# A second mixture of experts computed by tokens sorted into 15 blocks of one expert each

## The chip, the cores and the metric

The kernel runs on one core of one Trainium2 chip. The metric is the device time of one execution in microseconds (us). The kernel before was timed three times: 1374.06, 1376.27 and 1376.67 us, median 1376.27.

## The reference

Two transformer-like layers run over x of 8 batches, 512 tokens and 128 features, in float32. Each layer has a mixer and a mixture of experts, and in front of each stands a layer norm with a scale and a shift per batch. Layer 0 has causal attention (8 heads) and a small mixture (8 experts of 64). Layer 1 has a state-space mixer (a scan over 512 tokens, 256 channels, 16 states) and the mixture that the change is about, with 8 experts of 512:

```python
logits = xf @ gate_w                      # 128 -> 8 experts
top_w, top_idx = top_k(logits, 2)
top_w = softmax(top_w)
# per token: sum over its two experts e of
#   top_w * (gelu(xf @ w1[e] + b1[e]) @ w2[e] + b2[e])
x = x + gb * that_sum
```

Only two of the eight experts count for a token. Which two depends on the data.

## The kernel before

A batch of 512 tokens is the unit of work. Every engine has its order of work written out by hand. `main(b)` on TensorE is the attention of batch b (32 units of head and query tile), its attention output, layer 0's experts, and the projections and the short convolution of layer 1. `scan(b)` is the state-space scan. The experts of layer 1 belong to batch b-1 when `main(b)` and `scan(b)` run. They are cut into pieces and placed in the gaps, so each engine works on two batches at once (in `main(b)` also on the projections of b+1).

In the kernel before, every token passes through all 8 experts. `hid1(b, n)` (L598) is one hidden chunk: 128 features to 128 hidden units, all 512 tokens, 32 chunks in a batch. ScalarE takes it with a Gelu and its bias (`gelu1`, L929). `out1(b, n)` (L605) is one expert's output for one tile of 128 tokens, four products of 128x128x128, 32 of these in a batch. VectorE adds each output, times its gate, to `expert_sum` (`add_expert`, L1165, four at a time), and `finish` (L1177) multiplies with the layer's gate and adds the residual. A float32 product shows as two matmul records. All expert weights stay in SBUF; they are loaded once by ScalarE's DMA queue (`LATE`, L921).

The pieces lie in these places. In `main`, `early(e, ...)` puts hidden chunks and outputs between the steps of batch b. In `scan`, `SCAN_HIDDEN`, `SCAN_OUTPUT`, `SCAN_GELU` and `SCAN_ADD` name them by state. A Gelu among the scan's exponentials costs ScalarE two table loads (L1084, L1087). The router of batch b-1 runs inside the attention of batch b (`PE_HEAD`, `ACT_HEAD`, `DVE_HEAD` give its units).

In the scan VectorE does for each of 16 states two `tensor_tensor_scan` (L1482) and one product with C (`read_product`, L1156). It needs an exponential per half state from ScalarE (`decays`, L1074, three banks in a ring), an input product from GpSimd (`inject_state`, L435, three buffers), and a broadcast of C from TensorE (L872). GpSimd's products need B broadcast over all partitions: SyncE writes 16 rows to DRAM and reads them back broadcast, two states at a time (`spread_rows`, L395, three buffers). SyncE's queue also places the attention keys (`place_keys`, L372). GpSimd loads x, gates weights, sums half of the scan's output (L466) and stores the output.

After the last batch's scan nothing is left to run beside its experts: router, 32 hidden chunks and 32 outputs form a tail.

## Time and profile before

| What the page says | Value |
|---|---|
| runs | 1374.06 to 1376.67 us, median 1376.27 |
| span of the profiled execution | 1379.8 us |
| TensorE matmul busy | 1207.2 us, 87% |
| VectorE busy | 1037.0 us, 75% |
| ScalarE busy | 852.2 us, 62% |
| GpSimd busy | 489.3 us, 35% |
| moved by DMA | 53.22 MB, mean 39 GB/s |

The page has no time of its own for the profiled execution beside the span. Busy is the time in which an engine ran an instruction. The span covers the whole kernel, in which stages with different limits follow each other; eight batches make about seven equal periods with a head and a tail. Times in the rows below are us from the start of the span, unless a column says otherwise.

### The profile page before, as it was taken

The page shows a single profiled execution, that of the slowest core. Times are in us where ns is not written, and L with a number is a line of the kernel's source. Part 1 is how long each engine was busy: PE and PEld are TensorE (multiplying, and loading weights), DVE is VectorE, ACT ScalarE, POOL GpSimd, SP SyncE. Part 2 cuts the span into 40 slices and gives each one's busy share as a digit, 9 for nine tenths or more (in the row PEclk, how much of TensorE's full clock was granted, in tenths as well). Part 3 has the DMA queues.
Part 4 walks back from the last instruction along what each step waited for, and adds up shares of the span by engine and source line. Part 5 has one row for each costly group of instructions (what it writes and reads, how often), then busy time and mean ns, then how long its engine had stood idle before and what let it go on. Part 6 is the DMA issues. An engine that isn't in the chain of part 4 may idle for free. (4 is left out here: it accounts for less than half of the span.)

```text
span 1379.8 us, 19465 instructions
## 1 busy us (share of the span) xinstructions
PE 1207.2 (87%) x6560; PEld 760.5 (55%) x6560; DVE 1037.0 (75%) x2381; ACT 852.2 (62%) x1600; POOL 489.3 (35%) x309
## 2 busy tenths in 40 slices
PE   5974689989998889989999889989899899889698
PEld 3651145655665556555656456655656556555456
DVE  3666977599866997589866997579975998569822
ACT  2634446488646966489565866479664876469332
POOL 0103930078002950069100960049300870029300
PEclk8995579999999999999999999999999999999899
DMA  7101100030001200020001200021000300011000
GB/s 245 70 16 64 60 8 1 16 108 16 16 17 55 69 12 6 16 92 31 17 9 43 88 1 17 16 78 47 16 1 16 109 16 9 1 64 60 8 1 8
DMA packets 18514, 53.22 MB, mean 39 GB/s; under 512 B 4976, under 2 KB 5864, under 8 KB 18032
## 3 DMA queue, kind: packets, MB, share of 16 engines
q1 hardware_dynamic: 16112, 43.40, 9.8%
q0 software_dynamic: 1296, 4.20, 1.0%
q10 hardware_dynamic: 1008, 4.38, 0.8%
q8 instruction: 53, 0.87, 0.3%
q14 instruction: 45, 0.37, 0.1%
HBM read 45.40 MB, written 2.38 MB: 35 GB/s over the span
## 5 line engine op out<-in xcount | busy, mean ns | idle before, releaser
L1482 DVE TENSOR_TENSOR_SCAN probs_T<-bank,probs_T 128x512 f32<-128x512 f32 x256 | 303.9, 1212 | 16.1 <-ACT bank L1078 12.1
L618 PEld LDWEIGHTS bank<-w_w,hidden 128*128 128x128 f32 x2048 | 248.8, 192 | 72.9 <-issue 66.8
L602 PE MATMUL bank<-hT,w_w 128*128 128x512 f32 x512 | 262.9, 629 | 27.1 <-ACT hidden L933 26.2
L447 POOL TENSOR_TENSOR probs_T<-step_space,probs_T 128x1024 f32<-128x1024 f32 x120 | 282.2, 2358 | 5.9 <-DVE probs_T L1482 5.7
L618 PE MATMUL bank<-w_w,hidden 128*128 128x128 f32 x2048 | 251.6, 276 | 2.1 <-DVE expert_sum L1174 1.6
L933 ACT ACTIVATE hidden<-bank,w_b 128x512 f32<-128x512 f32 x256 | 169.6, 686 | 117.5 <-PE bank L602 116.9
L1006 ACT ACTIVATE probs<-bank,row_neg 128x128 f32<-128x128 f32 (+3 forms) x256 | 134.8, 528 | 151.7 <-DVE row_neg L1335 134.8
L1078 ACT ACTIVATE bank<-step_space,a_neg 128x512 f32<-128x512 f32 x256 | 167.8, 683 | 55.0 <-DVE probs_T L1482 36.7
L701 PE MATMUL bank<-k_pad,q_lat 128*128 128x512 f32 (+3 forms) x512 | 185.3, 448 | 5.8 <-DMA k_pad<-xc 5.8
L1335 DVE TENSOR_REDUCE row_neg<-bank 128x1 f32<-128x128 f32 (+3 forms) x256 | 123.5, 487 | 85.1 <-PE bank L703 82.7
L602 PEld LDWEIGHTS bank<-hT,w_w 128*128 128x128 f32 x512 | 89.0, 194 | 153.0 <-ACT hidden L933 97.0
L466 POOL TENSOR_TENSOR step_space<-step_space,probs 128x512 f32<-128x512 f32 x112 | 142.1, 1269 | 66.2 <-DVE probs L1162 66.1
L663 PE MATMUL bank<-probs,w_ident 128*128 128x512 f32 x256 | 146.0, 654 | 9.1 <-DVE probs L1162 9.1
L1162 DVE TENSOR_TENSOR probs<-probs_T,bank 128x1024 f32<-128x1024 f32 x128 | 153.2, 1197 | 0.4 <-PE bank L663 0.3
L711 PE MATMUL bank<-w_ident,probs 128*128 128x128 f32 x640 | 112.7, 278 | 8.6 <-DVE probs_T L1344 7.8
L1174 DVE SCALAR_TENSOR_TENSOR expert_sum<-bank,gates,expert_sum 128x128 f32<-128x128 f32 x256 | 71.4, 341 | 64.0 <-PE bank L618 62.5
L472 POOL TENSOR_TENSOR gated_out<-w_out_w,gate 128x256 f32<-128x256 f32 x8 | 5.8, 722 | 285.0 <-DVE xn L1214 285.0
L711 PEld LDWEIGHTS bank<-w_ident,probs 128*128 128x128 f32 x640 | 69.9, 142 | 59.1 <-issue 31.0
L872 PE MATMUL bank<-split,select 96*128 96x512 bf16 x128 | 52.7, 412 | 48.5 <-DVE probs L1162 45.7
L701 PEld LDWEIGHTS bank<-k_pad,q_lat 128*128 128x128 f32 x512 | 82.4, 200 | 14.8 <-issue 14.0
L982 ACT ACTIVATE probs_T<-bank 128x128 f32<-128x128 f32 (+3 forms) x176 | 73.8, 420 | 18.3 <-PE bank L711 17.5
L445 POOL TENSOR_TENSOR probs_T<-step_space,probs_T 128x512 f32<-128x512 f32 x16 | 23.3, 1459 | 169.3 <-DVE step_space L1471 169.3
(183 smaller groups left out, 1577.6 us busy)
## 6 DMA issues: line engine op xcount, KB each, us to landing
probs_T<-b_rows_dram SPq DMA_DIRECT2D x64, 512.0 KB, 3.7
w_w<-in_w_dram ACTq DMA_DIRECT2D x2, 2048.0 KB, 14.0
k_pad<-xc SPq DMA_DIRECT2D x64, 64.0 KB, 2.0
x_in<-in_x_dram POOLq DMA_DIRECT2D x8, 256.0 KB, 3.3
gate<-gate_rows_dram SPq DMA_DIRECT2D x1, 2048.0 KB, 7.0
out_dram<-x_out POOLq DMA_DIRECT2D x7, 256.0 KB, 2.8
step_space<-in_wmod_dram SPq DMA_DIRECT2D x1, 768.0 KB, 5.6
probs_T<-in_wqT_dram SPq DMA_DIRECT2D x1, 512.0 KB, 4.1
```

The source lines that it names most:

```text
L447: ins = nc.gpsimd.tensor_tensor(inject[:, n % 3, :, :], u[:], row.unsqueeze(1).to_broadcast([P, DH, T]), ALU.mult)
L466: ins = nc.gpsimd.tensor_tensor(state_sum[:, 1, :], state_sum[:, 1, :], read[:, n % 2, 1, :], ALU.add)
L602: mm(hid1_bank(n)[:], w["w1"][:, n // C1, n % C1 * P:(n % C1 + 1) * P], hT[3][:], start=True, stop=True).then_inc(hid1_mm.sem, 1)
L618: ins = mm(to[:, t * P:(t + 1) * P], hidden[:, (e * C1 + c) % (2 * C1), t * P:(t + 1) * P], w["w2"][:, e * C1 + c, :], start=(c == 0), sto ...
L663: mm(bank[SUM_BANK][:], ident[:], read[:, n % 2, 0, :], start=(n == 0), stop=(n == NS - 1)).then_inc(sum_mm.sem, 1)
L701: mm(s[:, 0:(i + 1) * P], q_lat[:, g, i * P:(i + 1) * P], k_pad[:, g, j, 0:(i + 1) * P], start=True, stop=False)
L711: ins = tr(bank[4 + n % 2][:, k * P:(k + 1) * P], probs_ring[:, n % 4, k * P:(k + 1) * P], ident[:])
L933: f(hidden[:, n % (2 * C1), :], hid1_bank(n)[:], ACT.Gelu, bias=w["b1"][:, n:n + 1]).then_inc(hid1_act.sem, 1)
L1006: f(probs_ring[:, n % 4, 0:(i + 1) * P], bank[SCORE_BANK[n % 4]][:, 0:(i + 1) * P], ACT.Exp, bias=row_neg[:, n % 4:n % 4 + 1], accum_out=r ...
L1078: f(decay(k)[:], delta[:, c, :], ACT.Exp, scale=a_neg[:, c, n:n + 1]).then_inc(dec_ok.sem, 1)
L1162: tt(read[:, n % 2, :, :], state[:, n % 2, :, :], bank[C_BANK][:].unsqueeze(1).to_broadcast([P, DH, T]), ALU.mult).then_inc(rd_ok.sem, 1)
L1482: v.tensor_tensor_scan(state[:, n % 2, c, :], decay(DH * n + c)[:], inject[:, n % 3, c, :], 0.0, ALU.mult, ALU.add).then_inc(st_ok.sem, 1)
```

## The change

The 512 tokens times two choices of a batch (1024 rows) are sorted by expert into blocks of 128 slots, each block belonging to one expert. Because each expert's rows are rounded up to whole blocks, 15 blocks are always enough (`NB = 2 * T // P + E - 1`), and all 15 are always computed.

- Router: `weigh` no longer forms gates for layer 1. TensorE counts ranks with five small bfloat16 products (a triangle and ones against the picks). VectorE's `give_slots` (12 small instructions, most of them waiting for the one before) turns ranks into a slot for each row, an expert for each block (`owner_int`) and a one-hot selection (`own`).
- GpSimd scatters the normalised rows with 8 indirect DMAs into `slots_dram` (`send_rows`). SyncE reads them back in 4 groups ("quads", `fetch_slots`). TensorE transposes a quad and ScalarE modulates it (`("quad", q)` of `FILLS`).
- For each block SyncE reads the expert's number into a register and fetches 512 KB of weights into a ring of 4 (`fetch_expert`; from the fifth block on it waits until the block that used the place is done).
- `fill` and `results` compute a block: a bias product in bfloat16 and 4 products 128x128x128, a Gelu over 128x512, a bias product and 4 products. ScalarE copies a quad of results to SBUF (`take_results`), and SyncE writes it to `results_dram` (`save_slots`).
- GpSimd gathers both rows of each token with 8 indirect DMAs (`collect_rows`) and combines them in 4 instructions (`combine`: 128x1024, then three of 128x512). For the last batch VectorE does this in two halves.
- Removed: `add_expert`, `finish`, the gate transposes and the b2 products (L652, L657), the copy L1322, the loads of w1 and w2 (4 MB), and the expert pieces between the first two projections of batch b+1.
- At the start: 8 new small weight arrays instead of b1 and b2, a memset and a DMA that clear `slots_dram` ahead of the first `place_keys`, and 15 small VectorE instructions in the set-up.

`_upto(n)` is the index behind block n in `FILLS`, and `_done(n)` is its `results`. The core of the diff, with indentation taken off and blank lines left out:

```diff
+def fetch_expert(b, n):
+    if n == 0:
+        sp.wait_ge(owner_ok.sem, owner_ok.at(b, 1))
+    if n >= WR:
+        sp.wait_ge(block_mm.sem, block_mm.at(b, n - WR + 1))
+    elif b > 0:
+        sp.wait_ge(block_mm.sem, block_mm.at(b - 1, NB))
+    e = sp.value_load(owner_int[0:1, n:n + 1], min_val=0, max_val=E - 1)
+    sp.dma_start(expert_w[:, n % WR, :],
+                 io["experts"][bass.ds(e, 1), :, :].rearrange("a p f -> (a p) f")
+                 ).then_inc(expert_in[n % WR].sem, 16)
...
+def start_experts(b):
+    for n in range(WR):
+        fetch_expert(b, n)
+    fetch_slots(b)
...
+if behind:
+    for n in SP_EXPERTS.get(p, ()):
+        fetch_expert(b - 1, n)
+    for q in SP_SAVES.get(p, ()):
+        save_slots(b - 1, q)
...
+def send_rows(b):
...
+for k in range(2):
+    for t in range(NT):
+        pool.indirect_dma_start(
+            out=slots_dram[:, :], out_offset=bass.IndirectOffsetOnAxis(ap=slot[:, k, t:t + 1], axis=0),
+            in_=xn_slots[:, t, :], in_offset=None).then_inc(spread.sem, 16)
...
+if b >= 2:
+    collect_rows(b - 2)
+if b < B - 1:
+    load(b + 1)
+if b >= 2:
+    combine(b - 2)
+    store(b - 2)
+send_rows(b - 1)
...
+    mm(to[:].rearrange("p (c s) -> p c s", c=C1), bias1[:],
+       own[:, n, :].unsqueeze(2).to_broadcast([96, C1, P]), start=True, stop=False, skip_group_check=True)
+    i = n % QUAD
+    for c in range(C1):
+        ins = mm(to[:, c * P:(c + 1) * P], expert_w[:, n % WR, c * P:(c + 1) * P],
+                 slots_T[:, n // QUAD % 2, i * P:(i + 1) * P], start=False, stop=(c == C1 - 1),
+                 skip_group_check=True)
+ins.then_inc(fill_mm.sem, 1)
...
+mm(to[:, i * P:(i + 1) * P], own[:, n, 0:1].to_broadcast([96, P]), bias2[:],
+   start=(i == 0), stop=False, skip_group_check=True)
 for c in range(C1):
-    ins = mm(to[:, t * P:(t + 1) * P], hidden[:, (e * C1 + c) % (2 * C1), t * P:(t + 1) * P],
-             w["w2"][:, e * C1 + c, :], start=(c == 0), stop=(c == C1 - 1))
-ins.then_inc(out1_mm.sem, 1)
+    ins = mm(to[:, i * P:(i + 1) * P], hidden[:, n % HR, c * P:(c + 1) * P],
+             expert_w[:, n % WR, F1 + c * P:F1 + (c + 1) * P], start=False, stop=(c == C1 - 1),
+             skip_group_check=True)
+ins.then_inc(block_mm.sem, 1)
...
+    ins = f_(slots_T[:, n % 2, 0:m], fill_bank(f)[:, 0:m], ACT.Identity,
+             bias=mod[:, 1, 3, bass.ds(b, 1)], scale=mod[:, 1, 4, bass.ds(b, 1)])
+else:
+    if n >= HR:
+        act.wait_ge(block_mm.sem, block_mm.at(b, n - HR + 1))
+    ins = f_(hidden[:, n % HR, :], fill_bank(f)[:], ACT.Gelu)
...
+def take_results(b, q, tail=False):
+    n = quad_size(q)
+    act.wait_ge(block_mm.sem, block_mm.at(b, q * QUAD + n))
+    if b > 0 or q >= 2:
+        act.wait_ge(saved[q % 2].sem, saved[q % 2].at(b, 16 * (q // 2)))
+    f_(slots_out[:, q % 2, 0:n * P], bank[TAIL_BANK[q] if tail else SLOT_BANK[q]][:, 0:n * P], ACT.Copy
+       ).then_inc(slots_done.sem, 1)
...
-stt(expert_sum[:, t, :], source[:, t * P:(t + 1) * P], gates[1][:, t, e:e + 1],
-    expert_sum[:, t, :], ALU.mult, ALU.add).then_inc(out1_add.sem, 1)
...
+link(tt(over[:], total.unsqueeze(2).to_broadcast([P, E, NT]),
+        limits[:].unsqueeze(1).to_broadcast([P, E, NT]), ALU.is_gt))
+link(v.reduce_sum(blocks[:], over[:], AX_X))
+link(v.tensor_tensor_scan(ends[:], w["unit"][:], blocks[:], 0.0, ALU.mult, ALU.add))
+mark(tt(starts[:], ends[:], blocks[:], ALU.subtract))
+link(tt(passed[:], ends[:, 0:E - 1].unsqueeze(1).to_broadcast([P, NB, E - 1]),
+        firsts[:].unsqueeze(2).to_broadcast([P, NB, E - 1]), ALU.is_le))
+mark(stt(place[:], starts[:].unsqueeze(1).to_broadcast([P, NT, E]), float(P), rank, ALU.mult, ALU.add))
+link(v.reduce_sum(owner[:], passed[:], AX_X))
+cp(owner_int[:], owner[:]).then_inc(owner_ok.sem, 1)
+link(tt(placed[:].rearrange("p k t e -> p k (t e)"), picks[:].rearrange("p k t e -> p k (t e)"),
+        place[:].rearrange("p t e -> p (t e)").unsqueeze(1).to_broadcast([P, 2, NT * E]), ALU.mult))
...
+FILLS = [("quad", 0)]
+for _n in range(NB):
+    FILLS.append(("block", _n))
+    if _n % QUAD == 1 and _n // QUAD + 1 < NQ:
+        FILLS.append(("quad", _n // QUAD + 1))
...
+PE_EARLY = (_fills(0, 3) + _done(0) + _fills(3, _upto(2)) + _done(1) + _fills(_upto(2), _upto(3)),
+            _done(2),
+            _fills(_upto(3), _upto(4)),
+            _done(3),
+            [],
+            _done(4) + _fills(_upto(4), _upto(6)))
+PE_SCAN = {1: _done(5) + _fills(_upto(6), _upto(7)), 2: _done(6) + _fills(_upto(7), _upto(8)),
+           4: _done(7) + _fills(_upto(8), _upto(9)), 5: _done(8) + _fills(_upto(9), _upto(10)),
+           7: _done(9) + _fills(_upto(10), _upto(11)), 8: _done(10) + _fills(_upto(11), _upto(12)),
+           10: _done(11) + _fills(_upto(12), _upto(13)), 11: _done(12) + _fills(_upto(13), _upto(14)),
+           13: _done(13), 14: _done(14)}
+ACT_EARLY = (_fills(0, _upto(3)), _fills(_upto(3), _upto(4)) + [("results", 0)])
+ACT_SCAN = {2: _fills(_upto(4), _upto(6)), 8: _fills(_upto(6), _upto(8)),
+            12: [("results", 1)], 14: _fills(_upto(8), _upto(10)), 20: _fills(_upto(10), _upto(12)),
+            24: [("results", 2)], 25: _fills(_upto(12), _upto(14)), 31: [("results", 3)]}
...
+SP_EXPERTS = {"head": (4, 5, 6, 7), 1: (8,), 3: (9,), 4: (10, 11), 5: (12,), 6: (13,), 7: (14,)}
+SP_SAVES = {1: (0,), 5: (1,), "end": (2, 3)}
```

`PE_EARLY[k]` stands where `early(...)` stood in `main`: 0 ahead of the third layer norm's transposes, 1 behind them, 2 in the middle of the four input projections, 3 behind them, 5 behind the dt products. `ACT_EARLY[0]` stands ahead of the third modulation, and `ACT_EARLY[1]` between the two `xi` and the two `res_gate` activations, ahead of their table load.

## Rows read from the trace of the kernel before

**Rows 1.** Windows of one steady period: us, busy per engine, clock, DMA share, GB/s.

```profile
600.60:662.30 61.70, 55.02 (x250) 33.59 (x250) 59.09 (x69) 51.60 (x66) 53.43 (x30) 0.97 0.14 49
662.30:706.50 44.20, 39.75 (x289) 26.78 (x288) 36.83 (x127) 27.62 (x94) 2.81 (x3) 1.00 0.04 13
706.50:738.90 32.40, 31.46 (x184) 20.16 (x184) 18.61 (x79) 13.86 (x22) 2.68 (x3) 1.00 0.07 18
738.90:759.00 20.10, 18.92 (x94) 12.14 (x92) 13.30 (x24) 14.73 (x23) 2.11 (x2) 1.00 0.21 63
```

**Rows 2.** Groups by line: out<-in, count, busy us, mean ns, idle before.

```profile
L1482 DVE TENSOR_TENSOR_SCAN probs_T<-bank,probs_T 128x512 f32<-128x512 f32 x256 | 303.9, 1212 | 16.1 <-ACT bank L1078 12.1 <-POOL probs_T L445 1.5 <-POOL probs_T L447 1.1
L447 POOL TENSOR_TENSOR probs_T<-step_space,probs_T 128x1024 f32<-128x1024 f32 x120 | 282.2, 2358 | 5.9 <-DVE probs_T L1482 5.7
L602 PE MATMUL bank<-hT,w_w 128*128 128x512 f32 x512 | 262.9, 629 | 27.1 <-ACT hidden L933 26.2 <-ACT hT L939 0.9
L618 PE MATMUL bank<-w_w,hidden 128*128 128x128 f32 x2048 | 251.6, 276 | 2.1 <-DVE expert_sum L1174 1.6
L933 ACT ACTIVATE hidden<-bank,w_b 128x512 f32<-128x512 f32 x256 | 169.6, 686 | 117.5 <-PE bank L602 116.9
L872 PE MATMUL bank<-split,select 96*128 96x512 bf16 x128 | 52.7, 412 | 48.5 <-DVE probs L1162 45.7 <-DVE split L1463 2.7
```

**Rows 3.** VectorE's timeline of one scan: start, us, line, instructions, idle before.

```profile
600.63 1.22 DVE L1482 TENSOR_TENSOR_SCAN probs_T<-bank,probs_T 128x512 f32<-128x512 f32 x1
...
603.18 1.10 DVE L1174 SCALAR_TENSOR_TENSOR expert_sum<-bank,gates,expert_sum 128x128 f32<-128x128 f32 x4
...
608.25 2.34 DVE L1482 TENSOR_TENSOR_SCAN probs_T<-bank,probs_T 128x512 f32<-128x512 f32 x2 [1.56 <-ACT bank L1078]
...
662.32 1.21 DVE L1162 TENSOR_TENSOR probs<-probs_T,bank 128x1024 f32<-128x1024 f32 x1
```

**Rows 4.** TensorE's granted clock early in that scan, columns as in rows 1.

```profile
604.00:606.00 2.00, 2.00 (x4) 0.68 (x3) 1.93 (x4) 1.16 (x2) 2.00 (x2) 0.54 0.33 127
```

**Rows 5.** Timeline of the attention: one of finish's two instructions, the b2 products.

```profile
668.66 0.68 DVE L1181 TENSOR_TENSOR expert_out<-expert_sum,gate 128x512 f32<-128x512 f32 x1
...
696.76 1.15 PE L657 MATMUL bank<-w_b,gates_T 8*128 8x128 f32 x8
```

**Rows 6.** TensorE's timeline: last projection, and the third layer norm's transposes.

```profile
729.10 1.00 PE L638 MATMUL bank<-w_wv_down,hT 128*128 128x64 f32 x8
...
738.90 0.60 PE L586 MATMUL bank<-w_ident,xn 128*128 128x128 f32 x4
```

**Rows 7.** ScalarE's timeline between the input projections and the convolution's output.

```profile
743.12 1.26 ACT L933 ACTIVATE hidden<-bank,w_b 128x512 f32<-128x512 f32 x2
744.39 1.28 ACT L1052 ACT_TABLE_LOAD   x1
...
747.21 1.23 ACT L1060 ACTIVATE xc<-probs_T 128x512 f32<-128x512 f32 x2 [0.25 <-DVE probs_T L1450]
```

**Rows 8.** DMA issues (KB each, us to landing), and GpSimd's time for an issue.

```profile
probs_T<-b_rows_dram SPq DMA_DIRECT2D x64, 512.0 KB, 3.7
out_dram<-x_out POOLq DMA_DIRECT2D x7, 256.0 KB, 2.8
...
L430 POOL DMA_DIRECT2D out_dram<-x_out x7 | 5.6, 796 | 37.3 <-DVE x_out L1184 37.3
```

**Rows 9.** The chain that ended last: start, us, what.

```profile
1309.56 3.78 PE bank L602 x4
...
1314.60 0.20 DVE logits L1222
...
1366.70 7.16 PE bank L618 x64
...
1375.70 0.72 POOL out_dram L523
```

**Rows 10.** TensorE's first score of batch 0.

```profile
28.78 0.76 PE L701 MATMUL bank<-k_pad,q_lat 128*128 128x128 f32 x2 [5.82 <-DMA k_pad<-xc]
```

More of the change, by code:

```diff
@@ L364, in build @@
         first_a, first_b = FIRST
-        then = [name for name in w if name not in LATE + first_a + first_b]
+        then = [name for name in w if name not in first_a + first_b]
         n_first, n_weights = len(first_a) + len(first_b), len(then)
@@ L622, in project, with pieces @@
+            def pieces(b, names, tail=False):
+                for kind, n in names:
+                    if kind == "fill":
+                        fill(b, n)
+                    else:
+                        results(b, n, tail)
             def project(b, k):
@@ new lines, in _upto, with _done @@
+def _upto(n):
+    return FILLS.index(("block", n)) + 1
+def _done(*blocks):
+    return [("results", n) for n in blocks]
+PE_EARLY = (_fills(0, 3) + _done(0) + _fills(3, _upto(2)) + _done(1) + _fills(_upto(2), _upto(3)),
[9 more added lines that the diff above has]
+           13: _done(13), 14: _done(14)}
```

559 lines of the change are left out of this document (340 added, 219 removed).

## The prediction

> **What bounds the kernel now.** I read the windows of one steady period first, then the groups by line, then the timelines of VectorE, TensorE and ScalarE in that period, the DMA issues, and last the chain at the end. The reader is to see in [rows 1] that the four stages have different limits. In the scan VectorE is busy 59.1 of 61.7 us, TensorE 55.0 and GpSimd 53.4. In the attention nobody is full (TensorE 39.8, VectorE 36.8 of 44.2): it is a chain from TensorE to VectorE to ScalarE and back. From 706.5 to 738.9 TensorE is full (31.5 of 32.4). The last 20.1 us are a serial chain into the next scan. A period is 158.4 us. In the tail TensorE is alone and full [rows 9].
>
> **The work saved, and why it is not the gain.** The dense experts cost TensorE (262.9 + 251.6) / 8 = 64.3 us a batch [rows 2]. The 15 blocks have 120 products of 128x128x128 at 251.6 / 1024 = 0.246 us, 29.5 us, with 15 wide and 15 narrow bias products (at most 0.41 and some 0.1 us, by L872) and 15 transposes (0.15 us each, by L586): 39 us. TensorE loses 25 us a batch. Gelus fall from 32 to 15 at 686 ns, with 8 quad passes added. The gain is only what lies on each stage's limit.
>
> **The scan.** VectorE loses six groups of four adds at 1.10 us [rows 3], five inside and one just ahead: 6.6 us. Given back: about 1.0, since GpSimd starts from the same operand and its first products (2.36 us, L447) now set the first states. At half state 2 ScalarE takes block 5, quad 2 and block 6 in one visit, but block 6 needs quad 2 modulated first, and TensorE's broadcast of C for state 0 is queued behind block 6. The sequence is a table load, Gelu, modulation, TensorE 1.2 us, Gelu, table load, against four Gelus before, where VectorE waited 1.56 us [rows 3]. TensorE also stands idle for some 6 us ahead of it, and the clock already dips there (0.54, [rows 4]). I take 2.5 us more wait. The visit at half state 14 has the same form one time more, 0.6. Net -2.5 us; bounds -6.6 (all hidden) and +1. GpSimd's 53.4 us of products and sums forbid much more.
>
> SyncE is in order: each row pair of B now stands behind fetches that wait for blocks. The worst is pair 4 behind experts 10 and 11 (block 7, placed at state 4). It would land about 13 us later than now, where GpSimd has some 11 us of slack, so GpSimd is 2 to 3 us late, which its lead over VectorE covers. At nothing, then, and 2 to 4 us a batch if the cover is gone.
>
> **Scan to attention.** The last group of adds (1.10) goes, but TensorE's last sum hides most of it: -0.4.
>
> **Attention.** Removed: finish (2 x 0.68), the b2 products (1.15, [rows 5]) and their copy (0.68). Added on VectorE: 12 small instructions at about 0.2, 2.4 us, all linked. On GpSimd, which is busy 2.8 of 44.2 us, 16 indirect DMAs and 6.2 us of combining (2.36 + 3 x 1.27). The router of the next batch waits for the gathers. These start when the scan's last sum is done, take 8 issues and 2 us of landing, and are needed some 22 us later. The scatter must be read back before TensorE's fills some 30 us after the slots. Both hold while an indirect issue costs under 2.5 us. Taken -1.0; bounds -3.2 and +2.4.
>
> **Main.** The two pairs of hidden chunks between the projections go, hidden by a layer norm: -0.5. Then TensorE had 9.8 us from L638 to L586 [rows 6]. New: a wait for v of 0.7, quad 0 and its modulation, blocks 0 to 3 with two results and quad 1: 0.44 + 1.1 + 4 x 1.11 + 2 x 0.95 + 0.44 and the waits give 738.9 again: 0. The layer norm was ready at 734.4, so what could be gained here is refilled.
>
> Then comes an added wait. ScalarE's `results 0` needs block 3, which TensorE does only behind all four input projections. Queued behind it are the silu table load (1.28), two `res_gate` and both `xc` activations, which everything up to the scan waits for. TensorE: projections 0, 1 to 742.2, block 4 to 743.3, projections 2, 3 to 745.1, block 3's results to 746.0. ScalarE: copy to 747.0, table to 748.2, res_gate to 749.5. So xc starts at 749.5, not 747.21, where the slack was 0.25 [rows 7]: +2.3. Bounds: 0 (if the convolution were later too) and +4 (expert 4's weights late at 742.2; they are asked for at about 735.3 and need 3.7 to land [rows 8] and a register read).
>
> A period: -2.5 - 0.4 - 1.0 - 0.5 + 2.3 = -2.1 us, and 7 such: -15 us. Bounds -6 and +2.5 a period.
>
> **The start.** Batch 0's first score waits 5.82 us for the keys [rows 10], whose DMAs stand behind SyncE's weight issues, slowed by the 4 MB of expert weights. These go; six more small arrays and a clear come. Bounds 0 and -5.8, taken -2.5.
>
> **The tail.** The router no longer stands behind two hidden chunks (3.78, [rows 9]): the logits come at 1310.8 instead of 1314.6. Choice 2.8, ranks 0.9, slots 2.1: 1316.6. Then 8 scatters. An indirect issue is nowhere in the trace; bounds 0.80 (GpSimd's issue of a direct one, [rows 8]) and 2.36 (its longest instruction, L447); I take 1.2, nearer the issue. Landing 2.0 (2.8 - 0.8). So 1328.3, read back 2.7: 1331. A block is 16 records at 7.16 / 64 = 0.112 [rows 9] and two biases, 2.1 us. Its weights are asked for when the block four earlier is done, and are needed two blocks later: about 0.9 of issue and register read plus 3.7 of landing over two blocks is 2.3 us each, 34.5 in all. With 2.5 to fill the pipeline and 2 for a low clock after TensorE's idle 15 us: 1370. Copy and save 3.0, gathers 9.6 + 2.0, two halves on VectorE 2 x 2.1: x_out at 1389 against 1375.5. So +13.5, bounds +7 and +38 (24 issues count, 8 of them an earlier batch's).
>
> **Sum.** 1376.3 - 15 - 2.5 + 13.5 = 1372. Durations are from the profiled execution, whose span is 1379.8, 3.5 us over the median of the runs; I carry differences to the median.
>
> **Rivals.**
>
> *The blocks pay more (chance 0.20).* If ScalarE's copy of quad 0 doesn't hold xc and the attention gains its full 3.2, a period gains 2.1 + 2.3 + 2.2 = 6.6 us, but GpSimd holds it to about 5.5: 1376 - 38 - 2.5 + 13.5 = 1349. For it: TensorE has slack everywhere, and its waits shape the attention. Against: the order of the copy is in the code.
>
> *The indirect DMAs are dear (0.18), slower.* Place: scatter and gathers of the tail. 16 issues are bare there, and 8 of the batch before stand ahead of the scatter. At 2.0 us each the tail is 13.5 + 16 x 0.8 + 6 = +32: 1391. It decides from about 1.45 us an issue. For it: each reads an index per row. Against: the direct issue of 512 rows is 0.80.
>
> *Weights or B rows come late (0.14), slower.* SyncE's register read before each fetch at 2 us instead of 0.5 gives the tail 0.75 x 11 = 8 us more, and stalls of 2 us a period in the scan: 1372 + 8 + 14 = 1394. For it: 512 KB take 3.7 us, and 15 fetches share one queue. Against: DMA share is 0.14 in the scan.
>
> *TensorE's clock (0.08), slower.* In the scan TensorE falls from 55 to some 36 busy us of 60, in lumps with idle between. At 1.2 GHz (half) that is 72 us, more than VectorE's. If a third of each scan ran so, states with a block would cost 1 us more, some 3 us a period: 1372 + 21 = 1393. Rows 4 show the clock at 0.54 right after one wait of 2.3 us, and back at 1.00 in the window of the scan (0.97 mean, [rows 1]). The Trainium skill, page "TensorE: Matmul & The Clock Gate", section "HAM oscillation", says that matmul groups shorter than the waits between them start cold each time. By that rule this rival holds in every scan and would take the 21 us; the trace agrees for the one wait only.
>
> **How the numbers follow.** Forecast 0.40 with its own range 1361 to 1383, then 0.20, 0.18, 0.14, 0.08. The range for 8 in 10 is 1346 to 1402. A measurement of this kernel tells 0.2% (2.75 us) from no change. Below 1373.5: 0.28 of the forecast and the first rival, 0.48. Within: 0.09 and 0.04 of the slower ones, 0.13. Above: 0.39.
>
> **What would show it.** Right: the scan's window at 57 to 60 us without L1174; xc starting right behind two res_gate and these behind the copy of quad 0, 2 us later than the convolution; about 17 us in the tail between slots and first fill; the last gathers 10 to 13 us. Wrong: a period shorter by over 5 us or longer at all; POOL indirect issues far from 1.2 us; SyncE waiting for blocks while GpSimd waits for rows; a clock under 0.9 in the scan.

## The result: 4.6% slower, and the profile after

The changed kernel takes 1442.3 us (median of five runs, 1431.0 to 1445.1) against 1376.3: ratio 1.0456, 95% interval 1.0413 to 1.0500. The forecast was 1372 and the range ended at 1402. The profiled execution is the quickest of the five: 1431.0 us, span 1429.2, mean granted TensorE clock 0.879 (before 0.950). In the other four the clock is 0.868 to 0.871. So the stages below add up to 49.4 us where the medians differ by 66.1: the span of 1379.8 is by itself 3.5 us over the median of the kernel before, and 1431.0 is 11.3 us under the median here. Each ratio further down is against the kernel before timed beside it (medians 1375.6 to 1378.9). One execution, of the kernel with both edits, took 1444.2 us at a clock of 0.778 and is left out of its ratio.

I cut both profiled spans at VectorE's own marks: x_mid, the first addition of the attention's output, the addition of out0, the first convolution tap, the first instruction on the x projection (split), the first scan. Sums over the kernel, in us:

| stage | before | after | difference | predicted |
|---|---|---|---|---|
| start to first scan | 128.6 | 119.5 | -9.1 | -2.5 |
| attention (x_mid to its first addition), 7 times | 264.8 | 289.9 | +25.1 | -7 |
| attention to out0, 7 | 140.8 | 145.2 | +4.4 | -3.5 |
| out0 to convolution, 7 | 90.8 | 90.7 | -0.1 | 0 |
| convolution to split, 7 | 57.5 | 76.0 | +18.5 | +16.1 |
| split to scan, 7 | 59.2 | 62.7 | +3.5 | 0 |
| scan to x_mid, 8 | 560.8 | 547.0 | -13.8 | -20.3 |
| x_mid to the end | 77.3 | 98.2 | +20.9 | +13.5 |
| span | 1379.8 | 1429.2 | +49.4 | -4 |

The worst term is the attention, 32 us from where I put it. Its first of the seven, with nothing to combine yet, takes 35.95 us; the other six take 41.0 to 42.8, where the kernel before has 38.0. First the windows of one steady period (us, busy time of each engine, granted clock, DMA share, GB/s), against [rows 1]:

```profile
604.30:665.20 60.90, 45.01 (x229) 30.98 (x229) 55.11 (x51) 42.95 (x60) 53.29 (x30) 0.89 0.35 122
665.20:713.00 47.80, 42.63 (x282) 28.94 (x282) 38.42 (x128) 26.64 (x89) 22.65 (x21) 0.89 0.21 66
713.00:745.60 32.60, 27.98 (x190) 20.39 (x189) 17.56 (x74) 11.20 (x18) 5.63 (x6) 0.95 0.26 75
745.60:768.10 22.50, 14.09 (x73) 8.98 (x71) 13.08 (x19) 14.48 (x22) 1.64 (x1) 1.00 0.45 153
```

The scan's window is 0.8 us shorter than before. The attention's is 3.6 us longer, although VectorE, TensorE and ScalarE do about the same work in it. What is new is GpSimd, 22.65 us busy instead of 2.81, and a clock of 0.89 instead of 1.00. Now VectorE's timeline there, and GpSimd's beside it (start, us, engine, line, instructions):

```profile
680.63 0.69 DVE L1546 TENSOR_REDUCE row_neg<-bank 128x1 f32<-128x512 f32 x1
681.24 0.63 DVE L1489 SCALAR_TENSOR_TENSOR rstd<-newton,rstd 128x4 f32<-128x4 f32 x1
681.90 3.23 DVE L1493 TENSOR_SCALAR xn_slots<-x_mid,meanvar,rstd 128x128 f32<-128x128 f32 x4
```

```profile
678.61 1.89 POOL L583 TENSOR_TENSOR rows<-rows,shares 128x1024 f32<-128x1024 f32 x1 [0.80 <-DMA rows<-results_dram,slot]
680.58 1.27 POOL L588 TENSOR_TENSOR rows<-rows 128x512 f32<-128x512 f32 x1
681.93 1.27 POOL L592 TENSOR_TENSOR x_out<-rows,gate 128x512 f32<-128x512 f32 x1
683.28 1.26 POOL L596 TENSOR_TENSOR x_out<-x_out,x_mid 128x512 f32<-128x512 f32 x1
```

In the kernel before the same step and the same normalisation were:

```profile
678.78 0.15 DVE L1280 SCALAR_TENSOR_TENSOR rstd<-newton,rstd 128x4 f32<-128x4 f32 x1
678.97 1.11 DVE L1283 TENSOR_SCALAR xn<-x_mid,meanvar,rstd 128x128 f32<-128x128 f32 x4
```

The four normalising instructions take 3.23 us instead of 1.11, exactly while GpSimd combines. Taken one by one they last 1.38, 1.42, 0.33 and 0.33: the first two end 0.08 us behind the ends of GpSimd's last two operations, and then the way is free. A step on 4 columns takes 0.63 instead of 0.15, and ends 0.02 behind the GpSimd operation beside it; one at 678.84 takes 1.68. The row maximum out of PSUM, in the same stretch, keeps its 0.69. TensorE waits for the normalised rows, and its clock falls behind the wait (windows of 4 us, same columns as above):

```profile
684.00:688.00 4.00, 1.52 (x10) 1.33 (x11) 3.97 (x11) 2.23 (x8) 1.37 (x2) 0.84 0.22 66
688.00:692.00 4.00, 4.00 (x22) 3.87 (x21) 0.99 (x3) 2.02 (x7) 0.00 (x0) 0.50 0.00 0
692.00:696.00 4.00, 4.00 (x32) 2.04 (x34) 2.83 (x15) 1.27 (x5) 0.00 (x0) 0.50 0.00 0
696.00:700.00 4.00, 4.00 (x37) 2.82 (x30) 2.85 (x12) 1.68 (x8) 0.00 (x0) 0.88 0.00 0
```

VectorE is full in the first window while TensorE works 1.52 of 4 us; for the next 8 us TensorE is full at 0.50 (1.2 GHz) and VectorE waits.

ScalarE behind the input projections, against [rows 7] (in brackets the idle time ahead and what ended it):

```profile
753.21 0.60 ACT L1112 ACTIVATE slots_out<-bank 128x512 f32<-128x512 f32 x1 [2.13 <-PE bank L805]
753.83 1.28 ACT L1230 ACT_TABLE_LOAD   x1
755.12 1.27 ACT L1233 ACTIVATE res_gate<-bank,w_in_b 128x512 f32<-128x512 f32 x2
756.28 1.15 ACT L1238 ACTIVATE xc<-probs_T 128x512 f32<-128x512 f32 x2
```

This is the copy of quad 0's results with the table load and the four activations queued behind it, as predicted. The new groups by line, against [rows 2] (out<-in, count, busy us, mean ns, idle before):

```profile
L1675 DVE TENSOR_TENSOR_SCAN probs_T<-bank,probs_T 128x512 f32<-128x512 f32 x256 | 301.2, 1211 | 39.0 <-ACT bank L1256 28.6 <-POOL probs_T L610 8.6 <-POOL probs_T L608 1.5
L610 POOL TENSOR_TENSOR probs_T<-step_space,probs_T 128x1024 f32<-128x1024 f32 x120 | 281.8, 2355 | 18.8 <-DMA probs_T<-b_rows_dram 16.2 <-DVE probs_T L1675 2.6
L575 POOL DMA_INDIRECT rows<-results_dram,slot x64 | 64.1, 1002 | 66.2 <-issue 66.2
L563 POOL DMA_INDIRECT slots_dram<-xn_slots,slot x64 | 63.0, 985 | 161.6 <-DVE slot L1452 121.1 <-issue 40.5
```

In the scan VectorE waits 39.0 us in all instead of 16.1, most of it for ScalarE's exponentials (28.6 instead of 12.1). GpSimd waits 16.2 us for rows of B, which I had covered "at nothing". An indirect issue is 1.0 us, with 0.30 before the next. Last the tail's chain and the end, against [rows 9], and the first score, against [rows 10]:

```profile
1356.22 2.23 DMA slots_dram<-xn_slots,slot
1358.47 2.83 DMA slots_in<-slots_dram
1361.34 1.13 PE bank L779 x4
...
1400.68 2.32 DMA results_dram<-slots_out
1403.00 1.92 issue
1404.92 0.98 POOL rows L575
...
1413.76 2.47 DMA rows<-results_dram,slot
...
1420.73 0.74 POOL out_dram L695
```

```profile
25.60 0.46 PE L894 MATMUL bank<-k_pad,q_lat 128*128 128x128 f32 x2 [2.59 <-DMA k_pad<-xc]
```

From the last store's issue to the end it is 8.5 us (1429.2 - 1420.7), where the kernel before needs 4.1 (1379.8 - 1375.7). The trace's records show where it goes: GpSimd's last instruction, a DRAIN, takes 5.87 us (1423.15 to 1429.02), and 1.46 in the kernel before.

### The profile page after: what moved, and what is told of

The parts are those of the page before. It is cut to its first block and busy times, and to the rows that moved or that the text cites. A ratio compares the mean times of both kernels' runs of the same rounds, so it can differ in the third digit from the quotient of the medians.

```text
span 1429.2 us, 19661 instructions
## 1 busy us (share of the span) xinstructions
PE 1073.9 (75%) x6224; PEld 728.4 (51%) x6224; DVE 1006.9 (70%) x2193; ACT 755.0 (53%) x1492; POOL 661.1 (46%) x466
## 5 line engine op out<-in xcount | busy, mean ns | idle before, releaser
L1675 DVE TENSOR_TENSOR_SCAN probs_T<-bank,probs_T 128x512 f32<-128x512 f32 x256 | 301.2, 1211 | 39.0 <-ACT bank L1256 28.6
L610 POOL TENSOR_TENSOR probs_T<-step_space,probs_T 128x1024 f32<-128x1024 f32 x120 | 281.8, 2355 | 18.8 <-DMA probs_T<-b_rows_dram 16.2
L1546 DVE TENSOR_REDUCE row_neg<-bank 128x1 f32<-128x128 f32 (+3 forms) x256 | 121.4, 485 | 80.1 <-PE bank L896 78.8
L858 PE MATMUL bank<-probs,w_ident 128*128 128x512 f32 x256 | 156.6, 697 | 9.1 <-DVE probs L1359 9.1
L629 POOL TENSOR_TENSOR step_space<-step_space,probs 128x512 f32<-128x512 f32 x112 | 142.2, 1269 | 40.4 <-DVE probs L1359 40.3
L805 PEld LDWEIGHTS bank<-expert_w,hidden 128*128 128x128 f32 x960 | 130.3, 211 | 33.4 <-issue 32.9
L805 PE MATMUL bank<-expert_w,hidden 128*128 128x128 f32 x960 | 147.1, 301 | 0.0
L790 PEld LDWEIGHTS bank<-slots_T,expert_w 128*128 128x128 f32 x960 | 136.3, 205 | 8.0 <-issue 2.3
L563 POOL DMA_INDIRECT slots_dram<-xn_slots,slot x64 | 63.0, 985 | 161.6 <-DVE slot L1452 121.1
L790 PE MATMUL bank<-slots_T,expert_w 128*128 128x128 f32 x960 | 135.4, 287 | 0.0
L904 PE MATMUL bank<-w_ident,probs 128*128 128x128 f32 x640 | 118.9, 290 | 20.3 <-DVE probs_T L1555 19.0
L1103 ACT ACTIVATE hidden<-bank 128x512 f32<-128x512 f32 x120 | 70.9, 597 | 84.3 <-PE bank L790 83.9
L1050 PEld LDWEIGHTS bank<-split,select 96*128 96x128 bf16 x128 | 13.0, 102 | 166.6 <-DVE probs L1359 162.9
L575 POOL DMA_INDIRECT rows<-results_dram,slot x64 | 64.1, 1002 | 66.2 <-issue 66.2
L786 PE MATMUL bank<-own,bias 96*128 96x512 bf16 x120 | 49.5, 412 | 59.4 <-ACT hidden L1103 50.1
```

What stands on the lines that cost most here:

```text
L610: ins = nc.gpsimd.tensor_tensor(inject[:, n % 3, :, :], u[:], row.unsqueeze(1).to_broadcast([P, DH, T]), ALU.mult)
L629: ins = nc.gpsimd.tensor_tensor(state_sum[:, 1, :], state_sum[:, 1, :], read[:, n % 2, 1, :], ALU.add)
L790: ins = mm(to[:, c * P:(c + 1) * P], expert_w[:, n % WR, c * P:(c + 1) * P], slots_T[:, n // QUAD % 2, i * P:(i + 1) * P], start=False, st ...
L805: ins = mm(to[:, i * P:(i + 1) * P], hidden[:, n % HR, c * P:(c + 1) * P], expert_w[:, n % WR, F1 + c * P:F1 + (c + 1) * P], start=False, ...
L858: mm(bank[SUM_BANK][:], ident[:], read[:, n % 2, 0, :], start=(n == 0), stop=(n == NS - 1)).then_inc(sum_mm.sem, 1)
L904: ins = tr(bank[4 + n % 2][:, k * P:(k + 1) * P], probs_ring[:, n % 4, k * P:(k + 1) * P], ident[:])
```

## The experiments

### GpSimd's combination against VectorE's normalisation

One wait is added in the changed kernel, so that the combination runs behind the normalisation:

```diff
                 if b >= 2:
+                    pool.wait_ge(*nth(ln_xn, b - 1, 3))
                     combine(b - 2)
```

> The changed kernel with one wait more: GpSimd combines the rows of the batch before (four tensor operations, 5.7 us) only after VectorE has normalised x_mid. Collision theory (VectorE's small norm steps and xn_slots are slowed while GpSimd's tensor operations run: xn_slots 3.23 us instead of 1.11, two norm steps 2.3 instead of 0.3, then a low TensorE clock behind the hole): the attention from x_mid to its end falls from 39.3 us to 35 or 36 in six batches, xn_slots is 1.1 us, ratio to the kernel before about 1.03 instead of 1.046. Rival (the attention is long because of the low clock, whose cause is TensorE's smaller load, or because of the gathers): the attention stays over 38 us and the ratio at 1.044 or above.

Measured: 1409.3 us, ratio 1.0204 (1.0162 to 1.0246), 33 us less. The attention is 35.5 to 36.1 us in batches 2 to 7, where it was 41.0 to 42.8: 38.7 us less in all six (the 39.3 of the expectation is no length by these marks), also less than the kernel before (37.98). VectorE and GpSimd there:

```profile
682.68 1.11 DVE L1494 TENSOR_SCALAR xn_slots<-x_mid,meanvar,rstd 128x128 f32<-128x128 f32 x4
```

```profile
683.88 1.89 POOL L583 TENSOR_TENSOR rows<-rows,shares 128x1024 f32<-128x1024 f32 x1 [4.05 <-DVE xn_slots L1494]
```

The same work 5 us later costs nothing. The reverse is the kernel before with such work added, and read by nobody:

```diff
+            def combine_pairs(b):
+                pool.wait_ge(chain_norm.sem, chain_norm.at(b, 7))
+                for k in range(4):
+                    pool.wait_ge(paired.sem, paired.at(b, k))
+                    nc.gpsimd.tensor_tensor(pair[:], pair[:], gate[:, b:b + 1, 3, :].to_broadcast([P, NT, P]),
+                                            ALU.mult if k % 2 == 0 else ALU.add).then_inc(paired.sem, 1)
```

> The kernel before, with four GpSimd tensor operations of 128x512 (1.27 us each) on a buffer of their own added in the attention of six batches, started when seven of the twelve norm steps of x_mid are done; nothing waits for their results. Collision theory: the normalisation (1.11 us) takes 2 to 3.3 us, small norm steps up to 1.7, and each of the six attentions grows by 2.5 to 4.5 us: ratio 1.011 to 1.02. Rival (GpSimd's tensor work costs VectorE nothing; the gathers or the blocks are the cause): ratio 0.998 to 1.002.

Measured: 1402.8 us, ratio 1.0184 (1.0156 to 1.0213). The six attentions grow by 5.1, 2.3, 4.5, 4.5, 2.3 and 4.5 us. Nothing of the blocks is in this kernel, and the normalisation takes the same 3.23 in each of the six:

```profile
686.16 3.23 DVE L1294 TENSOR_SCALAR xn<-x_mid,meanvar,rstd 128x128 f32<-128x128 f32 x4
```

So the same collision costs 2.3 us twice and 4.5 or more four times. The difference goes with TensorE's clock behind it, which stayed at 1.00 in the two and fell in the four. Batches 2 and 3 of this kernel (columns as in [rows 1]):

```profile
368.00:375.00 7.00, 6.47 (x69) 4.98 (x70) 4.83 (x23) 3.90 (x14) 0.00 (x0) 1.00 0.01 4
528.00:535.00 7.00, 6.73 (x35) 5.75 (x39) 3.05 (x13) 3.93 (x14) 0.00 (x0) 0.51 0.01 4
```

Two more runs of this kernel ask what collides. In one the wait is for `ln_xn` instead of the seventh norm step; in the other eleven memsets stand in place of the four operations:

```diff
-                pool.wait_ge(chain_norm.sem, chain_norm.at(b, 7))
+                pool.wait_ge(*nth(ln_xn, b, 3))
```

> The kernel before with the same four GpSimd tensor operations on a buffer of their own in six attentions, but started when x_mid is normalised, so that they stand beside VectorE's maxima and copies out of PSUM. Theory (it matters which VectorE operations stand beside): the normalisation takes 1.11 us, the maxima keep their 0.69 for 512 columns, the attention 37.98 us, ratio 0.998 to 1.003. Rival (any GpSimd work in the attention costs): 2 to 4 us in each of six attentions as in the run with the early start, ratio 1.009 or above.

```diff
-                for k in range(4):
+                for k in range(11):
                     pool.wait_ge(paired.sem, paired.at(b, k))
-                    nc.gpsimd.tensor_tensor(...)
+                    nc.gpsimd.memset(pair[:], 1.0).then_inc(paired.sem, 1)
```

> The kernel before with eleven GpSimd memsets of 128x512 (by the 1.73 us of the 1920-column one about 0.46 us each, 5 us in all) beside the norm steps, in place of the four tensor operations: GpSimd writes and reads nothing. Theory A (each of the four normalising operations waits for the whole GpSimd operation ahead of it, whatever that does): the normalisation takes up to 4 x 0.46 us more, about 2 to 2.9 us instead of 1.11, the 128x4 steps stay at 0.16 or wait up to 0.46; ratio 1.004 to 1.012. Theory B (only operations of GpSimd that read SBUF collide): normalisation 1.11 us, ratio 0.998 to 1.003.

Measured: 1.0003 (0.9982 to 1.0023) behind the normalisation, and 1.0004 (0.9979 to 1.0029) with memsets. VectorE behind the normalisation, with GpSimd at its four operations from 679.55 to 684.87:

```profile
679.38 0.68 DVE L1346 TENSOR_REDUCE row_neg<-bank 128x1 f32<-128x512 f32 x1
...
681.00 0.68 DVE L1355 COPY probs_T<-bank 128x512 f32<-128x512 f32 x1
...
682.37 1.30 DVE L1361 COPY hidden<-row_inv 128x256 f32<-128x256 f32 x1
```

Reads out of PSUM keep their time. The one copy out of SBUF takes 1.30 instead of 0.29, in a place where nobody waits for it. And the normalisation beside the memsets, then the memsets:

```profile
997.79 1.21 DVE L1293 TENSOR_SCALAR xn<-x_mid,meanvar,rstd 128x128 f32<-128x128 f32 x4
```

```profile
676.81 3.56 POOL L520 MEMSET pair<- 128x512 f32 x6 [2.00 <-DVE rstd L1286]
```

0.10 us more in each of the six, the steps on 4 columns keep their 0.15 or 0.16, and the attention is 38.06 us instead of 37.98. Theory B stands as to the cost: beside GpSimd operations that read the four lose 2.1 us, beside pure writes 0.1. They aren't untouched, though. The first and the third normalising instruction take 0.44 and 0.63 us instead of 0.34 and end 0.08 us behind the end of a memset (0.52 us each), but the instruction behind each is through 0.06 to 0.16 us later. The Trainium skill, page "SBUF — State Buffer", section "Who interferes with whom", says that VectorE's second pair of SBUF ports is also GpSimd's only one, that the first to issue holds it for its whole instruction, and that reductions never contend; the rows agree in that VectorE's held instructions end 0.02 to 0.08 us behind the end of a GpSimd operation, and in the 0.69 for the maxima. For a VectorE operation with two inputs in SBUF, as most of the small steps are, the section counts only a GpSimd operation that reads as a rival. For the 2-port modes, which tensor_scalar can enter (no row here shows the mode), it counts GpSimd whatever it does; beside pure writes the runs show 0.10 us, and that measurement decides here.

How much of the 6.6 us is the clock: two products that nothing reads, ahead of the transposes of xn_slots, with the collision left in.

```diff
+                    if behind and n == PE_HEAD[0]:
+                        for _ in range(2):
+                            mm(bank[MISC][:], ident[:], w["wfcT"][:], start=True, stop=True)
```

> The changed kernel, collision left in, with two 128x512 matrix products (0.94 us each) into an unused bank just ahead of the transposes of xn_slots, where TensorE idles 1.6 us. Clock theory (of the 6.6 us that the collision costs, the part beyond VectorE's lost 3.9 us comes from TensorE's granted clock falling to 0.50 behind that idle time): the clock in the 9 us behind stays above 0.9 and the attention falls from 42.5 to about 40 us; ratio about 1.035. Rival (the rest is the chain itself, the clock has no part): attention 42 to 43, ratio 1.043 or above.

Measured: 1436.6 us, ratio 1.0403 (1.0354 to 1.0453), too near the 1.0456 to be told from it. The attention is the cleaner number: 40.3 us in batches 3 to 6 instead of 42.5, with the clock at 0.96 and 0.62 where it was 0.50:

```profile
704.00:708.00 4.00, 2.68 (x21) 2.46 (x22) 2.48 (x8) 3.45 (x13) 0.00 (x0) 0.96 0.15 45
708.00:712.00 4.00, 4.00 (x40) 2.19 (x39) 2.61 (x13) 1.27 (x5) 0.00 (x0) 0.62 0.01 4
```

The two products aren't free: in batch 1, where nothing collides, the attention is 37.6 us instead of 35.95. So at least 2.2 of the 6.6 us are the clock, the same 2.2 by which the collision's price differs in the kernel before, and some 4 are VectorE's lost time (3.23 - 1.11, and two steps at 1.68 and 0.63 instead of 0.3 together, 4.1).

### The indirect DMAs

Eight indirect DMAs become two direct ones. The rows then go to and come from fixed places, so this kernel's experts see other rows.

```diff
-                    for t in range(NT):
-                        pool.indirect_dma_start(...).then_inc(spread.sem, 16)
+                    pool.dma_start(slots_dram[k * T:(k + 1) * T, :].rearrange("(t p) d -> p t d", p=P), xn_slots[:]
+                                   ).then_inc(spread.sem, 16)
```

> The changed kernel with every group of eight indirect DMAs replaced by two direct ones of the same bytes (rows go to and come from fixed places, so the experts see other rows). My theory: indirect issues cost time only where they are bare, in the tail: about 8 us less for the scatter and 8 less for the gathers, nothing in the periods, ratio about 1.034. If the 8.5 us from the last store's issue to the end (4.1 in the kernel before) come from the indirect DMAs, 4 us more go: 1.031. Rival (the gathers, 10 us of GpSimd in every period, slow the attention): 2 us or more less in each period too, ratio 1.024 or below.

Measured: 1403.2 us, ratio 1.0170 (1.0141 to 1.0199), 39 us less: my theory named 20, the rival's "2 us in each period" is nearer. But the gathers are not what slows the attention. Without their 10 us the combination falls onto other norm steps: xn_slots takes 1.12 us in every batch and the attention 38.4 in four of them, 2.5 more than without any collision. That is the collision again, half missed. In the tail the span ends 4.6 us behind the last store's issue instead of 8.5 (last line of its chain; the span is 1403.6):

```profile
1399.04 0.72 POOL out_dram L690
```

The tail from x_mid to the end is 82.7 us instead of 98.2. So 15.5 us of it are the indirect DMAs, of which 3.9 come at the very end of the program, where GpSimd's DRAIN takes 1.95 us instead of 5.87. I had no term for those.

### ScalarE's copy

```diff
-ACT_EARLY = (_fills(0, _upto(3)), _fills(_upto(3), _upto(4)) + [("results", 0)])
+ACT_EARLY = (_fills(0, _upto(3)), _fills(_upto(3), _upto(4)))
...
                     f(xc[:, c, :], conv[1][:, c, :], ACT.Silu).then_inc(xc_ok.sem, 1)
+                if behind:
+                    pieces(b - 1, [("results", 0)])
```

> The changed kernel with ScalarE's copy of the first quad's results moved from ahead of the silu table load to behind both xc activations. By the step of my prediction (2.3 us a period stand between convolution and scan because of this copy): convolution to split falls from 10.5 to 8.2 us in each of the periods with blocks, 14 to 16 us in all, ratio about 1.035. Rival (the copy only moves: TensorE's scan start waits for it as well): the stage split to scan grows by what the first loses, ratio 1.044 or above.

Measured: 1415.9 us, ratio 1.0301 (1.0239 to 1.0363), 26 us less. Convolution to split is 8.56 us in every batch instead of 10.44 to 11.91, which is 16 of it. The scan takes 1.1 us more. In the profiles, attention, attention to out0 and split to scan are 3.5, 3.7 and 3.6 us shorter too, though the edit doesn't touch them; their lengths follow the clock, as the next runs show. With both edits:

> Both edits of the two experiments before: the combination waits for the normalisation, and the first quad's results are copied behind xc. If the two are independent: attention 35.9 us in all six batches, convolution to split 8.56, and split to scan 8.44 throughout, since TensorE's idle time ahead of the x projection is 1.6 us instead of 3.8. From 1409: 7 times (11.3 - 8.6) and about four times 1.8 less, so about 1383, ratio 1.003 (0.998 to 1.010). Rival (what is shortened in one stage comes back in the next): over 1395, ratio 1.013 or above.

Measured: 1390.8 us, ratio 1.0088 (1.0057 to 1.0119); expected 1383. All three stages are at the times named (35.9, 8.56, 8.44), but attention to out0 is 21.8 us instead of 20.8 or 19.5, and the scan 69.1. A miss of a kind that the next runs explain.

### TensorE's clock

The stages between the attention and the scan have two or three lengths each: 19.5, 20.8 or 21.8; 8.44 or 10.23. In the kernel with the combination later, split to scan is 10.23 us in six batches, with these products in it:

```profile
755.49 3.78 PE L1038 MATMUL bank<-proj,w_dt_w 112*128 112x512 f32 x4 [0.78 <-ACT proj L1242]
```

In the profiled run of the changed kernel the same four took 1.99 us:

```profile
759.71 1.99 PE L1037 MATMUL bank<-proj,w_dt_w 112*128 112x512 f32 x4 [0.78 <-ACT proj L1241]
```

In both, TensorE had waited 3.78 us for xc; once the clock was at 1.00 behind it, once at 0.50. Three products into that wait:

```diff
                 early(3)
+                if behind:
+                    for _ in range(3):
+                        mm(bank[MISC][:], ident[:], w["wfcT"][:], start=True, stop=True)
```

> The kernel with the combination later, and in each batch three 128x512 matrix products (2.8 us) into an unused bank where TensorE waits 3.8 us for xc. Clock theory: the dt products (3.78 us at a granted clock of 0.50, 1.98 at 1.00) are always at 1.00, split to scan is 8.44 us in every batch instead of 10.23 in most, conversion to split about 10.4 instead of 11.5; 12 to 20 us less, ratio 1.007 to 1.012 instead of 1.020. Rival (added products delay the x projection or the clock falls all the same): ratio 1.018 or above.

Measured: 1391.1 us, ratio 1.0120 (1.0069 to 1.0170) against 1.0204 (1.0162 to 1.0246), two intervals that just touch: split to scan 8.44 us in seven of the eight batches, convolution to split 10.44 in all seven with blocks. This is also where I see the 11 us between the profiled run of the changed kernel and its median: that run has 8.44 in its first six batches and 10.23 in its last two, and the other runs' clocks are lower. The start can hold as much of it (see there). Their stages are not on record, so this is argued, not shown. Then products in such waits, on top of both edits: ahead of the second layer norm's transposes, of the x projection, of block 6 and of the first score, in this order in the diff:

```diff
+                    for _ in range(2):
+                        mm(bank[OUT_BANK][:], ident[:], w["wfcT"][:], start=True, stop=True)
...
+                for _ in range(1 if behind else 7):
+                    mm(bank[MISC][:], ident[:], w["wfcT"][:], start=True, stop=True)
...
+                    for _ in range(5):
+                        mm(bank[MISC][:], ident[:], w["wfcT"][:], start=True, stop=True)
+                    pieces(b - 1, _fills(_upto(6) - 1, _upto(6)))
...
+            for _ in range(3):
+                mm(bank[0][:], ident[:], hT[0][:], start=True, stop=True)
```

> The kernel with both edits (combination later, results copied behind xc), and 128x512 matrix products into unused banks where TensorE waits: two ahead of the second layer norm's transposes (wait 1.8 us), one ahead of the x projection (1.6), five ahead of block 6 (6.1), three at the start ahead of the first score, seven ahead of batch 0's x projection. Clock theory (what is still lost in the periods is lost at a granted clock of 0.50 behind these waits): attention to out0 19.5 instead of 21.8 in every batch, scan 67 to 68.5 instead of 69.1, first scan at about 119 to 121 instead of 127.9; a period 153.5 instead of 157; about 1361, ratio 0.985 to 0.990. Rival (the clock isn't held by this, or the products delay the real work): ratio 1.005 or above.

Measured: 1368.1 us, ratio 0.9936 (0.9919 to 0.9953). Attention to out0 is 19.48 us in batches 1 to 6 and the scan 67.8 in three of them; batch 7 stayed as it was (22.15), and in batches 2 and 6 the clock fell one stage later, where no products stand (out0 to convolution 14.81 us instead of 13.18), and the scan took 70.5. Hence less than hoped. The first scan came at 127.4 in this profile, of the longest of the seven executions (1377.2), but at 121.4 and 122.1 in the next two kernels, which have the same start. In the tail, twelve and then sixteen products, and the last store but one behind the scatter:

```diff
             expert_head(B - 1, 2)
+            for _ in range(12):
+                mm(bank[6][:], ident[:], w["wfcT"][:], start=True, stop=True)
             pieces(B - 1, TAIL, tail=True)
```

> As the kernel with products in all waits, and in the tail twelve more such products where TensorE waits 17 us for the scattered rows, and the last store but one behind the scatter instead of ahead of it. Clock theory: the first blocks of the tail run at 1.00 instead of 0.50 (4 us less), the scatter starts 0.8 us earlier: 4 to 5 us less than that kernel, ratio 0.982 to 0.987. Rival: the products last until after the rows are there, or the clock has fallen again: the same ratio within 0.002.

> The kernel with products in all waits and sixteen instead of twelve in the tail: the twelve ended 4.7 us before the scattered rows were there, and the granted clock was 0.50 to 0.75 again in the first 8 us of blocks. Clock theory: the wait left is under 1.5 us, the first blocks take 0.9 us of products each instead of 1.7, and the tail from x_mid to the end falls from 99.5 us to 95 to 96: ratio 0.990 to 0.994. Rival (the products run over the landing of the rows, or the tail's blocks are bound by the weights' fetches): tail 98 us or more, ratio 0.995 or above.

Measured: 0.9968 (0.9943 to 0.9994) and 0.9933 (0.9906 to 0.9960), 1369.3 and 1366.8 us. Twelve ended 4.7 us early and gained nothing: the tail was 99.4 us, and 99.2 without them. Sixteen end 1.4 us early, and the tail is 96.5 (the wait for the rows with sixteen):

```profile
1299.00 0.66 PE L780 MATMUL bank<-w_ident,slots_in 128*128 128x128 f32 x4 [1.43 <-DMA slots_in<-slots_dram]
```

The intervals of the three kernels overlap, so the tail's 3 us stand on single profiles.

### The start

In the kernel before, the 4 MB of expert weights go behind the first keys, and then three products into the wait for those keys:

```diff
-            for name in LATE:
-                act.dma_start(w[name][:], io[name]).then_inc(experts_in, 16)
...
                          .to_broadcast([P, B, 4, P])).then_inc(gates_spread, 16)
+            for name in LATE:
+                sp.dma_start(w[name][:], io[name]).then_inc(experts_in, 16)
```

> The kernel before with the two loads of all expert weights (4 MB) moved from ScalarE's queue at the start to SyncE's behind the placing of the first keys and the gates. Theory (the changed kernel's start gains 9 us because these loads no longer fill the DMA engines while the keys are placed, and because TensorE's clock no longer falls to 0.50 behind the wait for them): first score at 25 to 26 us instead of 28.8, first scan at 119 to 121 us instead of 128.6, all the rest as before; ratio 0.993 to 0.995. Rival (the gain has another source, such as the smaller set-up): ratio 0.998 or above.

> The kernel before with the expert weights loaded behind the first keys, and three 128x512 products into an unused bank where TensorE waits 2.6 us for those keys. Clock theory of the start: batch 0's attention runs at a granted clock of 1.00 in every run and the first scan starts at 119 to 120 us instead of 121.8; ratio 0.992 to 0.995, with less spread between runs. Rival (the low clock further on in batch 0 has another cause): ratio 0.996, as without the products.

Measured: 0.9955 (0.9929 to 0.9981), then 0.9943 (0.9924 to 0.9961). The first score is at 25.79 us instead of 28.78 and the first scan at 121.8 instead of 128.6:

```profile
25.79 0.46 PE L703 MATMUL bank<-k_pad,q_lat 128*128 128x128 f32 x2 [2.55 <-DMA k_pad<-xc]
```

So 3 us are the wait and 4 are what follows from it, in these two profiles. The products added nothing in the profile (first scan at 121.5); the two ratios can't be told apart.

The start isn't the same in every execution. The changed kernel and its six variants with the same start (each profiled once) have their first scan at 119.5, 127.8, 126.7, 119.5, 127.9, 133.0 and 122.2 us; the kernel before and the three with GpSimd work added have it at 128.6, 124.3, 128.8 and 128.9. In the profiled execution of the changed kernel the clock stays at 1.00 from 25 to 60 us; with the combination later, same start, it is 0.50 from 28 to 34.

## Why the prediction was wrong

**The step that failed** is the attention's: "On GpSimd, which is busy 2.8 of 44.2 us, 16 indirect DMAs and 6.2 us of combining". I priced this at nothing because GpSimd was free, and forecast -7 us for the seven attentions; they took 25.1 more. GpSimd was free, but its neighbour was not: VectorE had the small norm steps and the normalisation at that moment, and whichever came up beside a GpSimd operation ended only behind it (two steps and two of the four normalising instructions, 4.1 us in a batch). Behind that TensorE's clock fell, which is the other part of the 6.6. The two runs that move only this work (33 us less when it is later, 24 us more when it is added to the kernel before) show it from both sides. Without the collision the attention is 2.1 us shorter than before, inside my -3.2 to +2.4. I read an engine's idle share as permission, and did not ask what stood beside it on VectorE. The trace before had a hint. GpSimd's first product of a scan starts while VectorE works on delta in SBUF (L1467, 756.67 to 757.36), and takes 1.65 us where the second, beside a scan step, takes 1.26. No run tests this one:

```profile
756.83 1.65 POOL L445 TENSOR_TENSOR probs_T<-step_space,probs_T 128x512 f32<-128x512 f32 x1 [17.19 <-DVE step_space L1471]
759.11 1.26 POOL L445 TENSOR_TENSOR probs_T<-step_space,probs_T 128x512 f32<-128x512 f32 x1 [0.63 <-DVE step_space L1471]
```

**The clock** was a rival at 0.08, put into the scan at 21 us. The scan does run at a lower clock (0.89 instead of 0.97) and still got shorter, since VectorE bounds most of it; with the wait ahead of block 6 filled it gained 1.3 us in three batches (67.8 instead of 69.1). The clock costs where TensorE is on the path, behind waits of 1.6 to 3.8 us, in the attention, at out0 and at the dt products. The mechanism was on the list, its place and its chance were wrong. By the stages it is most of attention to out0 (+4.4 for -3.5) and all of split to scan (+3.5 for 0), both of which have their short length in some batches. Filling the waits took the kernel from 1.0088 to 0.9936. Two of the signs that I had named for being wrong came: a longer period (163.8 us by the windows instead of 158.4) and a clock under 0.9 in the scan.

**The copy on ScalarE**, +2.3 a period, was right to 0.1 us in the steady batches: res_gate starts right behind the copy and the table load, 2.2 us late by the split mark, and a run with the copy elsewhere gives 16 us back.

**The scan**: -2.0 a period where -2.9 was forecast (with the last group of adds). The wait ahead of block 6 is there (6.09 us of TensorE). The cover that I had assumed for late rows of B is not complete: 16.2 us of waits on GpSimd in eight batches, and VectorE's waits for GpSimd's products rise from 1.1 to 8.6. Its waits for ScalarE rise by 16.5 us, 2.4 a scan, where I had put 3.1.

**Out0 to convolution**: 0 forecast, -0.1 in all seven.

**The start**: -9.1, beyond my bound of -5.8, but this belongs to the one profiled execution. The wait gives 3.2 us (25.60 instead of 28.78). The rest goes with the clock in batch 0, 0.50 from 28 to 40 us in the kernel before and 1.00 here. Of the seven profiles above the middle one has its first scan at 126.7: -1.9, close to the -2.5.

**The tail**: +20.9 for +13.5. The indirect issue with its pause is 1.3 us where I took 1.2, and the fill of quad 0 starts 30.3 us behind x_mid, not 28.5. The blocks take 40 us, as I had 39. What I left out is the 3.9 us by which the span ends later with indirect DMAs in the program. The upper bound of +38 was also added up wrongly: 24 issues at 2.36 instead of 1.2 give 13.5 + 27.8 = +41.

**Rivals.** Dear indirect DMAs decide from 1.45 us an issue; it is 1.3, so this is no more than a part of the tail. Weights late: TensorE waits three times between blocks in the tail, 1.6 us in all.

## What to carry to other kernels

Before giving an idle GpSimd tensor work, look at what VectorE does in the same microseconds: beside reads out of PSUM it is free, beside a chain of operations on SBUF it can hold each one that comes up until the running GpSimd instruction ends. Then look at who waits for that chain, for TensorE's clock may fall behind a wait of two microseconds and double the price. Work taken off TensorE in a stage where it did not bind is paid back in clock if it leaves holes ahead of its critical products. The three mended forms of the changed kernel are 0.3 to 0.7% faster than the kernel before; with nothing but its start mended the kernel before gains 0.4 to 0.6%, so these runs show no gain of the blocks themselves.

## What the runs showed of the hardware

- GpSimd operations that read SBUF (1.27 us each) beside four VectorE tensor_scalar operations of 128x128 make them take 3.23 us instead of 1.11, by two that last until a GpSimd operation ends. GpSimd memsets of 0.52 us make them take 1.21. Reductions and copies out of PSUM keep their time.
- With 128 indirect DMAs in the program the span ends 8.5 us behind the issue of the last direct store, with none 4.6. All its data has moved by 2 us behind the issue. The time is in GpSimd's last DRAIN, 5.87 us with them and 1.95 without. Why it is longer is open.
- Behind the same wait of 3.78 us the granted clock was 1.00 in one run and 0.50 in another; stages then differ by 1.8 us in steps. The changed kernel and its variants spread by 6 to 20 us between executions, eight of ten by over 11, the kernel before by 6 to 12. That the spread comes from these waits is argued.
- The same collision of GpSimd and VectorE in the attention cost 2.3 us where the granted clock stayed at 1.00 behind it, and 4.5 where it fell to 0.51.
